# Three spare comparison matrices a group instead of four, and a fifth layer with split neighbour rows

## The reference, cut to what matters

```python
def _sage_conv(x, src, dst, Wl, bl, Wr):
    msg_sum = segment_sum(x[src], dst, N);  deg = segment_sum(ones, dst, N)
    return msg_sum / max(deg, 1)[:, None] @ Wl + bl + x @ Wr
h  = relu(_sage_conv(x, ...))                       # layer a1, 128 -> 128
x1 = layernorm(x + _sage_conv(h, ...))              # layer a2, 128 -> 128
g1 = relu(_sage_conv(x1, ...))                      # layer b1, 128 -> 256
g2 = relu(_sage_conv(g1, ...))                      # layer b2, 256 -> 256
out = layernorm(x1 + _sage_conv(g2, ...))           # layer b3, 256 -> 128
```

## Time and profile before

| what | us |
|---|---|
| median of three runs (lowest, highest) | 5212.95 (5212.83, 5214.96) |
| the profiled execution | 5213.1 |
| its span in the profile | 5211.5 |
| busy in the span: TensorE, VectorE, ScalarE, GpSimd | 4970.9, 3692.6, 2554.6, 2342.6 |
| layers begin at about (first gather): a1, a2, b1, b2, b3 | 135, 770, 1583, 2527, 4009 |

### The profile page before, as it was taken

One profiled execution on the slowest core, in us unless ns is written; L12 is line 12 of the kernel. 1 busy time (PEld: TensorE's weight loads), 2 busy tenths in 40 slices (PEclk: granted clock), 3 DMA queues, 4 the chain that ended last, 5 costly groups with the idle time before them and its releaser, 6 DMA issues. The chain is left out here.

```text
span 5211.5 us, 156564 instructions
## 1 busy us (share of the span) xinstructions
PE 4970.9 (95%) x42398; PEld 4907.3 (94%) x42399; DVE 3692.6 (71%) x10002; ACT 2554.6 (49%) x7254; POOL 2342.6 (45%) x2947
## 2 busy tenths in 40 slices
PE   1899989999998999999899999999998999999999
PEld 0788889999998999999899999999998999999999
DVE  4688877888887999999666666767675555555555
ACT  0455547777774333333333333333333666666666
POOL 1788866666644444444332323222222444444441
PEclk9999999999998999999999999999999999999999
DMA  1677777888875655665555555555555766666665
GB/s 29 172 211 210 208 198 210 229 229 228 229 224 160 196 193 196 197 196 194 167 173 179 173 179 173 178 174 178 174 177 162 222 216 219 219 217 219 219 216 186
DMA packets 1247576, 1007.06 MB, mean 193 GB/s; under 512 B 70406, under 2 KB 1178275, under 8 KB 1247492
## 3 DMA queue, kind: packets, MB, share of 16 engines
q1 hardware_dynamic: 1171780, 825.23, 51.2%
q0 software_dynamic: 75712, 180.76, 11.4%
HBM read 645.58 MB, written 360.13 MB: 193 GB/s over the span
## 5 line engine op out<-in xcount | busy, mean ns | idle before, releaser
L1206 PE MATMUL f_product_b<-f_ring_b,f_onehot_b 128*128 x6272 | 997.2, 281 | 0.0
L1206 PEld LDWEIGHTS f_product_b<-f_ring_b,f_onehot_b 128*128 128x128 f32 x6272 | 856.3, 189 | 0.0
L778 PE MATMUL m_product_a<-m_ring_a,m_onehot_a 128*128 x4704 | 846.9, 291 | 0.0
L1262 ACT ACTIVATE f_ring_b<-f_e_product_b,t_rec_all 128x256 f32 (+1 forms) x784 | 329.4, 471 | 1010.0 <-PE f_e_product_b L1219 1010.0
L1200 PE MATMUL f_product_b<-b_r_all,f_t_hi_b 128*128 128x256 f32 x2352 | 723.1, 307 | 0.0
L901 DVE TENSOR_TENSOR m_onehot_b<-iota_all,t_win_all 128x512 f32<-128x512 f32 x392 | 269.6, 688 | 557.3 <-PE m_product_b L778 557.3
L1202 PE MATMUL f_product_b<-b_r_all,f_t_lo_b 128*128 128x256 f32 x2352 | 661.2, 281 | 0.0
L1201 PE MATMUL f_product_b<-b_r_all,f_t_hi_b 128*128 128x256 f32 x2352 | 659.6, 280 | 0.0
L778 PEld LDWEIGHTS m_product_a<-m_ring_a,m_onehot_a 128*128 128x128 f32 x4704 | 651.9, 192 | 0.0
L1139 POOL TENSOR_TENSOR f_held_b<-ones_all 1x1 f32<-1x1 f32 x390 | 71.5, 183 | 1243.0 <-ACT f_e_idx_b L1244 1152.6
L901 DVE TENSOR_TENSOR m_onehot_a<-iota_all,t_win_all 128x512 fp32r<-128x512 f32 (+1 forms) x784 | 536.8, 686 | 102.7 <-PE m_product_a L778 94.0
(11 more groups left out here) (197 smaller groups left out, 12292.7 us busy)
## 6 DMA issues: line engine op xcount, KB each, us to landing
g<-f_rows_out_b SPq DMA_DIRECT2D x392, 512.0 KB
f_rows_in_b<-g SPq DMA_DIRECT2D x196, 512.0 KB, 4.1
m_rows_in_b<-g SPq DMA_DIRECT2D x196, 512.0 KB
m_t_full_a<-in_x_flat_dram SPq DMA_DIRECT2D x196, 256.0 KB
h<-m_rows_out_a SPq DMA_DIRECT2D x196, 256.0 KB
m_rows_in_a<-h SPq DMA_DIRECT2D x196, 256.0 KB
m_res_in_a<-in_x_dram SPq DMA_DIRECT2D x196, 256.0 KB, 3.1
x<-m_rows_out_a SPq DMA_DIRECT2D x196, 256.0 KB
```

The source lines that it names most:

```text
L778: mm = pe.matmul(both, onehot[:, s, n, :], ring[:, bass.ds(at[n] * (C * fo), C * fo)], start=False, stop=(w == 1), skip_group_check=True)
L1206: mm = pe.matmul(to, onehot[:, s, n, :], ring[:, bass.ds(at[n] * (2 * fo) + half * fo, fo)], start=False, stop=(w == 1 and half == 1))
```

## The change

It changes four things.

1. **Seven windows a group instead of eight** (all layers). Each node tile has one first window; three extra windows a group go to whichever tiles run on into a second edge tile. The output place of an extra matmul comes from a register too, so `places` reads ten numbers instead of eight. The second `compare` makes three matrices instead of four. `window_tables` computes the choice with more small VectorE instructions.
2. **The wide pass** follows the narrow one's loop (`phased`), gathers six pairs ahead, holds its products in two two-bank tiles with one semaphore count a group, and does both halves of `add_up` in the step after.
3. **Layer b3** gets `split=True, shared=2`: the split ring with `low_part`, `ring_low` and `mix`, and two of the four normalising instructions on VectorE (`normalise_rest`).
4. **`normalise_rest`** stands directly behind `offset`, ahead of the second `compare`.

```diff
@@ class/constants
+FIRSTS, EXTRAS = T, 3
+WINDOWS = FIRSTS + EXTRAS
+PLACES = WINDOWS + EXTRAS
@@ window_tables
-        LAST = 16 + 4 * B
+        LAST = 31 + 4 * B * T
...
@@ narrow_pass, multiply
-                    for w in range(2):
-                        n = 2 * t + w
-                        mm = pe.matmul(both, onehot[:, s, n, :], ring[:, bass.ds(at[n] * (C * fo), C * fo)],
-                                       start=False, stop=(w == 1), skip_group_check=True)
+                    pe.matmul(both, onehot[:, s, t, :], ring[:, bass.ds(at[t] * (C * fo), C * fo)],
+                              start=False, stop=False, skip_group_check=True)
                 if u == 1:
+                    wait(pe, s_onehot, g.n(0, 2) + 2)
+                    for n in range(FIRSTS, WINDOWS):
+                        mm = pe.matmul(product[s][:, bass.ds(at[n + EXTRAS] * (C * fo), C * fo)], onehot[:, s, n, :],
+                                       ring[:, bass.ds(at[n] * (C * fo), C * fo)],
+                                       start=False, stop=True, skip_group_check=True)
                     mm.then_inc(s_product.sem, 1)
@@ narrow_pass, VectorE step
                 if norm and has(g, 2):
                     offset(g.plus(-2))
+                if shared and has(g, 2):
+                    normalise_rest(g.plus(-2))
                 if not is_last(g):
                     compare(g.plus(1), 1)
                 if split and q is not None:
                     ring_low(q)
-                if shared and has(g, 2):
-                    normalise_rest(g.plus(-2))
@@ wide_pass, TensorE multiply
-                wait(pe, s_sum, g * U + u - 3)
-                bank = product[s * U + u]
+                    wait(pe, s_sum, g.n(-1, U))
+                bank = product[s]
@@ wide_pass, VectorE step
                 if not is_last(g):
-                    nodes_lo(g + 1, 1 - s)
+                    nodes_lo(g.plus(1))
                 if has(g, 1):
-                    add_up(g - 1, 1 - s, i - 1 + s, 1)
+                    add_up(g.plus(-1), 0)
                 if not is_last(g):
-                    compare(g + 1, 1 - s, 0)
-                    compare(g + 1, 1 - s, 1)
-                add_up(g, s, i, 0)
+                    compare(g.plus(1), 0)
+                if has(g, 1):
+                    add_up(g.plus(-1), 1)
+                if not is_last(g):
+                    compare(g.plus(1), 1)
@@ build
-            dict(name="b3", h=g2, out=o2, relu=True, w=2, f_out=128, turned=False, Wl=b_wl3, Wr=b_wr3, b=b_b3,
+            dict(name="b3", h=g2, out=o2, relu=True, w=2, f_out=128, turned=False, split=True, shared=2, Wl=b_wl3, Wr=b_wr3, b=b_b3,
                  res=x1),
```

More of the change, by code:

```diff
@@ L42, in __init__ @@
         self.slots = self.groups * T
-        self.block = max(n for n in range(1, P + 1) if self.slots % n == 0)
         self.names = {}
@@ L485, in wait @@
         eng.wait_ge(counter.sem, counter.at(k))
-def pairs(eng, first, end, body):
-    turns = (end - first) // 3
-    if turns > 0:
-        with eng.Fori(0, turns) as turn:
-            for n in range(3):
-                body(turn * 3 + (first + n))
-    for i in range(first + 3 * turns, end):
-        body(i)
-def steps(pr, eng, step):
-    G, L = pr.groups, LEAD // 2
-    for p in range(LEAD):
-        step(None, p, p % 2, None, p // 2)
-    for g in (0, 1):
-        step(g, g + LEAD, g, 0, L)
-    def pair(i):
-        for s in range(2):
-            step(i * 2 + s, i * 2 + (s + LEAD), s, i, i + L)
-    pairs(eng, 1, G // 2 - L - 1, pair)
-    for g in (G - LEAD - 2, G - LEAD - 1):
-        step(g, g + LEAD, g % 2, g // 2, g // 2 + L)
-    for g in range(G - LEAD, G):
-        step(g, None, g % 2, g // 2, None)
 class At:
@@ L1131, in _ @@
+            phased(pr, sp, step)
+            store(At(G - 1))
             for s in range(2):
@@ L1273, in step @@
                 if g is not None and not is_last(g):
-                    nodes_hi(g + 1, 1 - s)
+                    nodes_hi(g.plus(1))
                 q = turned_before(g, p)
                 if q is not None:
-                    ring_hi(q, 1 - s)
-            for p in range(2):
-                take_numbers(p, p)
-            steps(pr, act, step)
+                    ring_hi(q)
+            for p in range(D):
+                take_numbers(At(p))
+            phased(pr, act, step)
         @block.vector
```

425 lines of the change are left out of this document (240 added, 185 removed).

## The result

The kernel after takes 6101.5 us (median of four runs, 6091.7 to 6117.3) against 5214.0 us: ratio 1.170, 95% interval 1.168 to 1.173. The forecast was 5336 us, in a range of 5150 to 5420. The direction was right, and the time lies far outside the range. Its profiled execution spans 6115.7 us, 904.2 more than the one before.

What follows compares the result with a forecast made beforehand. It took TensorE to bound a2, b1, b2 and b3, GpSimd a1, and after the change a ring of waits b3: 5213.1 - 45 - 46 - 46 - 8 + 5 + 2 + 1 + 260 = 5336 us, range 5150 to 5420.

Steps and rivals of the forecast that it cites:

- part 1: Seven windows, a1 to b2: fewer TensorE records, -45 us in a2, -46 each in b1 and b2, -8 in a1.
- the start: Ahead of a1's first gather: more count and small instructions in `window_tables`, +5 us.
- the +2: Wide pass, b1 and b2 together: more gather pairs asked for at the start, +2 us, ends -5 and +6.
- the register instructions show: Rival, a2, b1 and b2: window register instructions not hidden, 0.28 us a group, +165 us; chance 0.03 shared with the clock.
- a1: -8: Layer a1: one record fewer, but GpSimd's gathers set the pace; -8 us, ends 0 and -25.
- b2: -46: Layer b2: two TensorE records fewer a group, 0.233 us each group, -46 us.
- The wide pass's sums: Wide pass: VectorE's two sums ready at 3.7 us of a 4.45 us step, hidden; +118 us at most in b1.
- The ring: Layer b3: waits through ScalarE, GpSimd's gathers, `mix` and VectorE close after one step, 7.48 us; layer +260 us.
- GpSimd's 3.40 us: Term of b3's ring of waits: from the end of `take_numbers` to the second gather's end, 3.40 us.
- TensorE's bound in b3: Rival: b3's ring of waits is broken and TensorE sets the step, -178 us, total 4898 us; chance 0.12.
- the quick `mix`: Rival, b3: `mix` at its low end, ring of waits 6.55 us, total 5164 us, faster; chance 0.08.
- The clock: Rival, b3: TensorE's clock falls in new gaps, +771 us, total 5836 us; chance 0.03 shared with the registers.

Runs made afterwards that it cites:

- e3: Kernel after with table rows of twelve words, all twelve read by each load: 5365.1 us, ratio 1.029 to the kernel before.
- e4: Kernel after with the three column numbers packed into the eighth word, so rows and loads of eight words: 5368.7 us, ratio 1.030.
- e13: Kernel after with table rows of twelve words, of which each load reads ten: ratio 1.041, on a slower chip.
- e12: Kernel before with only the change's split last layer, `normalise_rest` directly behind the shift: 5436.9 us, ratio 1.043.
- e11: e3's kernel with `normalise_rest` moved behind `ring_low`: 5379.2 us, ratio 1.032.
- e1: Kernel before with each load reading ten words instead of eight, rows still eight words apart: 5405.1 us, ratio 1.037.
- e17: e6's kernel with `normalise_rest` behind `ring_low`: 5084.5 us, ratio 0.975.
- e16: e6's kernel repeated unchanged on a faster chip: 5034.6 us, ratio 0.966.
- e6: e3's kernel with `mix` ahead of the gathers in GpSimd's step: ratio 0.969, on the slower chip.
- e14: e6's kernel repeated unchanged on the slower chip: ratio 0.971.

## Why the prediction was wrong

**The step that failed** is in part 1: "A window's register instruction takes 46 ns on TensorE's queue; an extra one needs a second for the output place. Even three times 46 ns is under the 0.23 us of its two records: nothing, and if that cover is gone, at most 6 x 0.046 = 0.28 us a group." It priced the instructions that use the register values, and left out the one that fetches them. That one was in the trace of before, 980 times, at 0.587 us or more, longer than any register instruction beside it. The change made it read ten words at 40 bytes apart. The 46 ns were right for a first window; an extra one has a single instruction of 74 to 79 ns, less than two of 46. The load went from 0.59 us to 1.07 and 2.4 to 3.5 us in turn. Mending the table took back 736 us of the 765 by which the result exceeded the forecast. That e3's 5365 us lie only 29 above the forecast is luck in part: against their terms a1 came 28 us, b2 49, a2 8 and the start 3 too high, b1 4 and b3 53 too low, and the +2 doesn't show. The rival "the register instructions show" (+165) was in the neighbourhood but priced by the same row, so its range couldn't hold what came.

**Parts 1 and 2 with the load mended (e3).** a2: forecast -45, measured -37. b1: -46, measured -50. a1: -8, measured +20; the view of its waits has TensorE waiting 51.8 us in 78 groups for `m_ring_a`, for which it didn't wait before, and what makes that late was not tried. It isn't the 0.84 us load: with e4's 0.59 us the layer measures +27. b2: -46, measured +3. There the gap ahead of the first weight load of a step gives the reason, 25.6 us in 800 (2900 to 3700 us of e3):

```profile
L1200 PEld LDWEIGHTS f_turned_b<-ident_all,f_rows_in_b 128*128 128x128 f32 x849 | 90.8, 140 | 25.6 <-issue 24.0
```

0.24 us in each of 107 steps, 47 us in 196, about what the two records fewer should have won. With e13's load of 1.07 us the gap is 0.47 us (48.4 us, 104 times in 800), so beyond the cover each 0.23 us of load costs as much. With the 0.59 us load of e4 the gap is 0.14 us (15.2 us in 108 steps) and the layer measures -15; the kernel before had no gap with that load, and whether the unpacking or the shorter step leaves this rest was not tried. So the cover for the load is thin, and its size is the term to check. The wide pass's sums stayed hidden, as forecast. `window_tables`: +5 forecast, +8 measured.

**Part 3.** The ring is there as the prediction traced it. Its forecast was 7.48 us a step; measured 7.14 (84 steps in 600 us), and b3 +208 us instead of +261. `mix` was forecast at 1.24 us, between ends of 0.61 and 1.67, and takes 1.28. The term that was mis-sized is GpSimd's 3.40 us. In the kernel after the ring takes 7.40 to 7.47 us in three groups of each six, as forecast, and 6.77 to 6.79 us in the other three. In these the gap behind the mark is 0.15 and the first gather 1.03 us, instead of 0.49 and 1.3 us. The row was no odd one out: in the kernel before, all 165 steps of b3 between 4100 and 5100 us have 0.48 and 1.28 to 1.31 us there, while its a1 has 0.15 and 1.03 us (400 to 460 us). So the term changed with the change, in three of each six groups; e12, with the old table and eight matrices, shows the same two kinds of step. What makes a step one or the other is open. The estimate from the Trainium skill (GPSIMD Engine Reference, "Performance versus the Vector engine"), 1.12 us for the sum, is 13% under the measured 1.28. Part 4, forecast at nothing, is worth some 14 us in this ring (e11).

**The rivals.** TensorE's bound in b3, the quick `mix`: both dead by the ring's rows. The clock: dismissed with a chance of 0.03 that it shared with the registers, and it did fall, not in b3, where it was feared, but in a1, where the loads made gaps that were not foreseen: 84 us.

**What spoke of the load ahead of time.** The Trainium skill, Runtime: NRT & Kernel Launch, section "Instruction fetch mechanics", puts a load of registers, there from HBM, at about 200 ns a register "even for bulk". For this table in SBUF the rows come near it off the boundary (1.94 us for eight words, 0.24 each) and for 16-bit words (0.236 each); not for whole 16-byte pieces, where eight words take 0.587 us, 0.073 each. The measurement decides: there is a bulk rate, and the kernel before had it.

## What to carry to other kernels

When a change widens something that is read into registers, price the read itself, from its row, and look at how the new shape lies: 32-bit words, rows that begin on 16 bytes, whole pieces of four, with padding read along if need be. Where work is handed to another engine, follow the waits round until they close, and check the order in that engine's queue: the piece that others wait for goes ahead of the piece that only feeds later steps. A term of such a ring that the kernel before shows, even in every step, can come out otherwise when the order around it changes: give it a range down to the shortest that any layer shows.

## What the runs showed of the hardware

- A load of register values on TensorE's queue took, at its shortest: 8 words on a 16-byte boundary 0.587 us, 12 words 0.844, 10 words 1.071; 8 words off the boundary 1.94, 16 words of 16 bits 3.783. The differences are 0.26 us for a piece of four (0.844 - 0.587) and 0.24 us for a single word ((1.071 - 0.587) / 2).
- Loads stretched beyond that in some layers of some kernels: ten aligned words to 1.94 us (median) in b1 of e1, but 1.07 to 1.10 in b1 of e13; ten unaligned words up to 3.5 us, against at most 2.42 in b3 of the kernel after (5200 to 5280 us); eight aligned words to 1.04 in a1 of the kernel before. What makes the difference stays open.
- In b2 a load of 0.59 us left no gap in the kernel before and 0.14 us a step in e4; 0.84 us left 0.24 (e3) and 1.07 us 0.47 (e13).
- While GpSimd's 1.37 us sum over SBUF ran, a VectorE instruction of 0.34 us from SBUF to SBUF that started 0.16 us behind it took 1.30 us, and ended 0.1 us after it. The other way round, where VectorE's comparison had started 0.10 us ahead of the sum (e17), the comparison kept its 0.55 us and the sum took 1.58 instead of 1.28 us. The Trainium skill, SBUF — State Buffer, section "Who interferes with whom", has VectorE and GpSimd share one pair of ports as an exclusive lock that the first to start keeps for its whole instruction, where VectorE's instruction is of a kind that uses the pair; the rows agree.
- Two chips ran the same kernel before in 5213 to 5215 us and a third in 5333 to 5338 us; the ratio of one changed kernel differs by 0.3 to 0.5% between them (e16 0.966, e6 0.969, e14 0.971). Its a1 took 653 us on a faster chip (e16) and 747 and 758 us on the slower one (e6, e14).
